# Filler matmuls in the light steps of a scan, a third slot for spread step sizes, and a reordered opening, in a language-model tower on one core

## The reference

```python
emb = tok_table[token_ids] + seg_table[segment_ids] + pos_table
h = layernorm(emb) * gamma + beta
x = layernorm(h)
# mamba block on x, h = h + block(x)
u = rmsnorm(x) * w_norm1
z = (u @ W_in.T) * sigmoid(u @ W_gate.T)
dt_in, Bm, Cm = split(z @ W_xproj.T, [96, 16, 16])
dt = softplus(dt_in @ W_dt.T + b_dt)
A_bar = exp(dt[..., None] * A);  Bx = (dt * z)[..., None] * Bm[:, :, None, :]
hs[t] = A_bar[t] * hs[t - 1] + Bx[t]          # along the 128 tokens, 384 channels x 16 states
y = sum_s(hs * Cm) + D_skip * z
x = x + y @ W_out.T
x = x + (silu(hf @ W_gate_ffn.T) * (hf @ W_up.T)) @ W_down.T       # hf = rmsnorm(x) * w
```

## Time and profile before

| what | us |
|---|---|
| three timed runs, median | 1767.92 |
| lowest and highest of them | 1763.59, 1771.11 |
| the profiled execution | 1750.55 |
| its span in the trace | 1748.8 |

### The profile page before, as it was taken

How to read it: one execution, slowest core, us unless ns; L and a number is a source line. 1 busy time by engine, 2 the same in 40 slices (tenths; PEclk the granted TensorE clock), 3 DMA queues, 4 the chain that set the end, 5 groups by cost and what they waited for, 6 DMA issues and landing times.

```text
span 1748.8 us, 22815 instructions
## 1 busy us (share of the span) xinstructions
PE 1333.2 (76%) x7000; PEld 914.0 (52%) x7000; DVE 807.0 (46%) x1503; ACT 522.6 (30%) x881; POOL 523.0 (30%) x421
## 2 busy tenths in 40 slices
PE   0437578889978776599994778989998889999960
PEld 0211123234233345499993564756657488888850
DVE  2337898776788664111111636355463422222212
ACT  0154455754744411133331213415151101001000
POOL 4645575644663561100113400000000600000025
PEclk9855677968787877799997668898988899999985
DMA  4233353442443312888982100000000388888843
GB/s 118 43 102 85 85 142 96 123 109 73 115 120 97 84 41 64 259 271 273 273 276 91 46 1 0 1 0 0 0 1 6 114 234 238 225 231 240 222 128 94
DMA packets 71612, 206.41 MB, mean 118 GB/s; under 512 B 11360, under 2 KB 32608, under 8 KB 66752
## 3 DMA queue, kind: packets, MB, share of 16 engines
q1 hardware_dynamic: 59648, 181.28, 37.3%
q0 software_dynamic: 11904, 24.40, 4.7%
HBM read 183.42 MB, written 22.22 MB: 118 GB/s over the span
## 4 chain that ended last, share of the span: by engine, by line
PE 43%; DMA 16%; DVE 15%; issue 9%; POOL 5%; ACT 4%; DVEq 2%; POOLq 2%; SPq 1%; ACTq 1%
PE ps L825 31%; DMA expert<-arena 13%; DVE arena L1479 4%; PE ps L956 3%; PE ps L1182 3%; POOL arena L546 2%; PE ps L970 1%; DMA arena<-sorted 1%; DMA arena<-dt 1%; PE ps L1174 1%; DVEq L1475 1%; DVE ps L1474 1%; ACT arena L687 1%; POOL h_rows L377 1%; PE ps L820 1%
## 5 line engine op out<-in xcount | busy, mean ns | idle before, releaser
L1479 DVE TENSOR_TENSOR_SCAN arena<-arena,ps 128x1024 f32<-128x1024 f32 x96 | 219.5, 2287 | 34.2 <-ACT arena L687 19.8
L825 PE MATMUL ps<-arena 96*128 96x128 f32 (+1 forms) x1680 | 222.5, 289 | 9.3 <-issue 8.2
L825 PE MATMUL ps<-xTF,wreg 96*128 96x512 f32 x352 | 217.3, 767 | 8.5 <-DVE arena L1648 4.6
L825 PEld LDWEIGHTS ps<-arena 96*128 96x128 f32 (+1 forms) x1680 | 213.6, 191 | 13.7 <-issue 13.7
L956 PE MATMUL ps<-arena,pick 32*128 32x512 f32 x384 | 134.6, 805 | 109.3 <-DVE arena L1479 97.7
L534 POOL DMA_DIRECT2D expert<-arena x88 | 47.7, 542 | 487.4 <-DVE arena L1608 268.1
L412 POOL DMA_INDIRECT sorted<-x_rows,row_i x64 | 62.8, 981 | 413.4 <-DVEq L1395 394.6
L687 ACT ACTIVATE arena<-arena,wreg 128x508 f32<-128x508 f32 x192 | 127.2, 710 | 118.5 <-DVE arena L1479 56.4
L825 PE MATMUL ps<-arena,ew_in 96*128 96x128 f32 x1248 | 150.0, 278 | 8.1 <-issue 7.8
L825 PEld LDWEIGHTS ps<-arena,ew_in 96*128 96x128 f32 x1248 | 145.6, 194 | 12.0 <-issue 11.9
L1474 DVE TENSOR_TENSOR ps<-ps,arena 128x1024 f32<-128x1024 f32 x96 | 117.1, 1219 | 73.9 <-PE ps L956 72.2
(11 more groups left out here) (208 smaller groups left out, 1723.6 us busy)
## 6 DMA issues: line engine op xcount, KB each, us to landing
arena<-dt SPq DMA_DIRECT2D x96, 512.0 KB, 4.6
ew_in<-in_e_in SPq DMA_DIRECT2D x24, 768.0 KB, 6.5
arena<-in_e_in SPq DMA_DIRECT2D x24, 768.0 KB, 6.2
ew_out<-in_e_out SPq DMA_DIRECT2D x20, 675.0 KB, 6.9
arena<-in_e_out SPq DMA_DIRECT2D x20, 675.0 KB, 7.1
...
```

What stands on the lines that cost most here:

```text
L825: last = pe.matmul(o, lhs, rhs, start=(n == 0), stop=(n == len(pairs) - 1))
L1479: ve.tensor_tensor_scan(hid[k % 3], dec[k % 3], bx.rearrange("p x t -> p (x t)"), 0.0, ALU.mult, ALU.add)\
```

## The change

Fillers: behind the jobs of a step, `keep_busy` counts what the step has on TensorE by a table of costs and adds matmuls of the identity with 256 columns of constants, up to 7 units; the results go to the bank of the next job and nobody reads them. A third `raw` slot lies in the upper half of what had been scratch (`ew_in_all[1]`), whose scratch tiles move up and get narrower. In chunk 0, VectorE multiplies z by the gate straight from PSUM, and ScalarE's copy and POOL's multiply go. POOL fetches chunk 1's rows at the start, and chunk 3's one tile at a time in steps 0 to 3. VectorE gets the mean square of the normalized rows as variance / (variance + eps), with no moments of their own. The embedding of chunks 2 and 3 stands at later steps, `embed_rows` of each chunk by itself.

```diff
-        raw = [part(18432, 1024), part(19456, 1024)]
+        raw = [part(18432, 1024), part(19456, 1024), ew_in_all[1][:, 0:1024]]
...
-        def rt(n, words=256):
-            return ew_in_all[1][:, 256 * n:256 * n + words]
+        def rt(n, words=192):
+            return ew_in_all[1][:, 1024 + 192 * n:1024 + 192 * n + words]
...
-                if k >= 2:
-                    sp.wait_ge(s_dec, 2 * (k - 1))
-                sp.dma_start(raw[k % 2], dt_rows[c][4 * g + i, half:half + 1].broadcast_to((NST, 8, 2 * CN))).then_inc(s_raw[k % 2], 16)
+                if k >= 3:
+                    sp.wait_ge(s_dec, 2 * (k - 2))
+                sp.dma_start(raw[k % 3], dt_rows[c][4 * g + i, half:half + 1].broadcast_to((NST, 8, 2 * CN))).then_inc(s_raw[k % 3], 16)
...
             embed(0)
+            embed(1)
             pool.wait_ge(s_sm, 4 * 16)
...
             embed_beta(0)
-            embed(1)
-            embed(2)
             pool.wait_ge(s_emb[1], 2 * CT * 16)
             embed_sum(1)
             embed_pos(1)
-            embed(3)
+            embed(2)
             pool.wait_ge(s_fn, 2)
             embed_gamma(1)
             embed_beta(1)
-            for g in range(DG):
-                gate_z(0, g)
...
                     if c == 0:
-                        if n == 1:
+                        if n < CT:
+                            embed(3, (n,))
+                        if n == 5:
                             pool.wait_ge(s_emb[2], 4 * CT * 16)
                             embed_sum(2)
-                        if n == 2:
+                        if n == 6:
                             embed_pos(2)
-                        if n == 3:
+                        if n == 8:
                             embed_sum(3)
-                        if n == 4:
+                        if n == 11:
                             embed_pos(3)
-                        if n == 8:
+                        if n == 14:
                             pool.wait_ge(s_fn, NCH)
                             embed_gamma(2)
-                        if n == 9:
+                        if n == 15:
                             embed_beta(2)
-                        if n == 10:
+                        if n == 20:
                             embed_gamma(3)
-                        if n == 11:
+                        if n == 21:
                             embed_beta(3)
...
             for job, _ in opening[:12]:
-                work(job)
+                if job[0] != "ez":
+                    work(job)
...
+            cost = dict(eturn=1, egate=4, ez=4, elow=6, edt=2, ebc=2, lout=6, lturn=1, lgate=4, lup=4, ldown=8, lnext=1, lrout=4,
+                        lscore=1, rank=1)
+            order = [(c, n, job) for c in range(NCH) for n in range(PAIRS) for job in work_at(c, n)]
+
+            def keep_busy(c, n, todo):
+
+                left = [job for cc, nn, job in order if (cc, nn) > (c, n)]
+                units = 7 - 2 - (2 if n % 2 else 0) - sum(cost[job[0]] for job in todo)
+                if not left or units <= 0:
+                    return
+                b = seat(*left[0])
+                for _ in range(units):
+                    pe.matmul(ps[:, b, 0:2 * P], ident, cst[:, 0:2 * P], start=True, stop=True)
...
                 for job in todo[1:]:
                     work(job)
+                keep_busy(c, n, todo)
...
-                norm(x, h_rows[:, c * CT:(c + n) * CT, :], LN_EPS, n=n * CT)
-                ve.drain()
-                moments(x, n * CT)
-                rstd(x_rms[:, c * CT:(c + n) * CT], n * CT, RMS_EPS, True)
+                m = n * CT
+                norm(x, h_rows[:, c * CT:(c + n) * CT, :], LN_EPS, n=m)
+                ve.drain()
+                ve.tensor_tensor(tt[:, 0:m], yy[:, 0:m], yy[:, 0:m], ALU.mult)
+                ve.drain()
+                ve.tensor_tensor(mv[:, 0:m, 1], tt[:, 0:m], mv[:, 0:m, 1], ALU.mult)
+                ve.drain()
+                rstd(x_rms[:, c * CT:(c + n) * CT], m, RMS_EPS, False)
...
+            for g in range(DG):
+                bank, n = seats["ez", 0, g]
+                ve.wait_ge(s_sig, g + 1)
+                ve.wait_ge(s_wfull[bank], n + 1)
+                ve.tensor_tensor(zT[0][:, g, :], ps[:, bank, :], tA[:, g, :], ALU.mult).then_inc(s_wfree[bank], 1)
+                ve.drain().then_inc(s_z, 1)
             embed_norm(1, 1)
             embed_rows(1, 1)
...
-                if k == 6:
+                if k == 12:
                     embed_norm(2, 2)
-                if k == 14:
-                    embed_rows(2, 2)
+                if k == 18:
+                    embed_rows(2, 1)
+                if k == PAIRS + 2:
+                    embed_rows(3, 1)
```

More of the change, by code:

```diff
@@ L203, in tower @@
         s_uf, s_dec, s_scan, s_hc, s_sum = [sem(n) for n in ("s_uf", "s_dec", "s_scan", "s_hc", "s_sum")]
[L204 removed]
+        s_raw, s_dtw = [sem(f"s_raw{k}") for k in range(3)], [sem(f"s_dtw{g}") for g in range(DG)]
         s_yT, s_yfree = sem("s_yT"), sem("s_yfree")
@@ L374, in _, with embed @@
             pool.wait_ge(s_idx, 32)
-            def embed(c):
-                for t in range(c * CT, (c + 1) * CT):
+            def embed(c, tiles=range(CT)):
+                for t in [c * CT + j for j in tiles]:
                     pool.indirect_dma_start(h_rows[:, t, :], None, tok_tab, bass.IndirectOffsetOnAxis(tok_i[:, t:t + 1], 0))\
```

7 lines of the change are left out of this document (3 added, 4 removed).

## The result

| | before | after |
|---|---|---|
| median of 20 runs each, us | 1768.22 | 1757.01 |
| lowest, highest | 1753.81, 1778.72 | 1738.46, 1769.39 |
| profiled execution, its span | 1750.55, 1748.8 | 1742.62, 1740.9 |
| first scan starts at | 113.51 | 99.75 |
| from scan 0 to scan 31 | 157.7 | 162.8 |

The ratio is 0.9939 [0.991, 0.9967]: 11 us faster, where 1756 was forecast. The traces agree with the sum: the last scan starts 10.5 us earlier, and the terms of the forecast (all of them up to that scan) gave -12.

What follows compares the result with a forecast made beforehand. The prediction saw no one bound: opening, VectorE's embedding stretches and TensorE's falling clock each had their own. Terms -17 + 3 + 6 - 4 = -12 us gave 1756 us against the 1767.92 median, range 1738 to 1773.

Steps and rivals of the forecast that it cites:

- Opening: Before the first scan: it starts 17 us earlier; ends -15 with `elow` at 1.2 GHz, -10 if POOL comes late.
- The part on z: Opening: z on VectorE behind each projection lets ScalarE take `elow` at 68.3 instead of 86.14, -17.8 us.
- row fetches: +2.3: Opening, POOL: chunk 1's fetches move ahead of chunk 0's sum, which starts 2.3 us later.
- mean square: -1.4: Opening, VectorE: three small operations taking 0.7 us replace moments and follow-up of 2.15 us, -1.4.
- Stretches: Embedding arithmetic between scans on VectorE: one norm, 10.0, and two row parts, 20.2, instead of 27.0 us: +3.2.
- Fillers and waits of steps 0 to 31: Chunk 0's scan: VectorE's waits sum to 28 us against 21.9, +6; ends 12 (-10) and 45 (+23).
- the clock falls anyway: Scan: each VectorE stretch still leaves TensorE idle for some 8 us, so its clock drops despite fillers.
- my case: The forecast itself: terms sum to -12 us, 1756 us, with TensorE's clock still falling behind VectorE's stretches; chance 0.46.
- rival 1: Scan: the clock holds, waits shrink to 12, softplus chain gains 8; middle -27 us, 1741; chance 0.22.
- rival 3: Light steps of chunk 0 and the last chunk: fillers at 1.2 GHz cost 25 us, +13 overall, 1781; chance 0.11.
- The other chunks' fillers: Chunks 1 to 3: few light steps, hidden by the stretches just before them; taken at nothing.
- the third slot: ScalarE's waits for spreads before the softplus, chunks 1 and 2 (1.84, 2.01 us), go: -4; ends 0 and -8.

Runs made afterwards that it cites:

- z_only: The kernel before with only z multiplied by its gate on VectorE straight from PSUM; one run, 1761.49 us.
- m_moments: The changed kernel with the moments of the normalized rows computed again; one run, 1763.68 us.
- f_nowait: The changed kernel without fillers in steps 16, 18 and 20 of chunks 1 and 2; ratio to before 0.9937 [0.9897, 0.9977].
- b_fillonly: The kernel before with only the fillers added; ratio to before 0.9879 [0.98, 0.9957], 4 runs, median 1752.92 us.
- l_first: The changed kernel without the three fillers ahead of step 3; one run, 1778.36 us.
- h_steps: The changed kernel with POOL's fetches, sums and positions reordered, norm behind step 8, both row parts in one stretch behind step 14; one run, 1739.83 us.
- c_rawtwo: The changed kernel with two slots for spread step sizes again; ratio to before 0.9951 [0.9922, 0.9979].

## Why the forecast was right, and where it was right by luck

**Opening (-17; measured -13.8).** The part on z was right: z_only has its first scan at 95.95, 17.6 us earlier (forecast 17.8), and `elow` at 2.4 GHz took 2.84 us. The step that failed is "row fetches: +2.3" with "mean square: -1.4", together 0.9 for the start of TensorE; its first projection came 4.4 us later. The fetches did cost 2.45 on POOL, but the position pass then came 2.68 instead of 0.82 behind the sum, +1.9. The mean square did save 1.5 (m_moments). But with chunk 1's rows there early, POOL's position pass over them fell on VectorE's chain and held one operation, 1.46 us for 0.17 (the row at 41.95), +1.3. That is 2.45 + 1.9 + 1.3 - 1.5, or 4.1 of the 4.4. Both surcharges had been put at nothing. The size of the first is in part chance: the gap is 1.47 to 3.46 us in the seven kernels with all eight fetches ahead of the sum, so the -13.8 of this trace was -11.7 to -14.4 in kernels with the same opening.

**Stretches (+3.2; measured +12.8).** The step that failed was to count the arithmetic only. Unheld, the three stretches would be 14.7 - 5.8 = 9.0, 13.5 - 4.1 = 9.4 and 11.5 - 2.0 = 9.5, together 27.9, even below the 30.2 that I took. What I left out is whom VectorE meets there: 5.8 us of waiting for POOL, whose passes I read as moved but not against VectorE's new step, and 6.1 us of held operations. The row of 2.16 us beside 2.35 had shown the second. By the rule of the Trainium skill's page the sum was to be 4 us worse; measured was 6.1 us, so the rule was nearer than leaving it out.

**Fillers and waits of steps 0 to 31 (+6; measured -7.7).** 162.8 - 108.8 - 39.8 = 14.2 us of waits, against 21.9 before and 28 forecast. By place: steps 3 to 6 4.8 (forecast 12), 7 to 12 0.2 (2), after step 12 1.2 (5), interval 18 and on 4.5 (2.5), after step 26 3.4 (6.5). The prices of one filler, 0.46 and 0.91, held. What failed is "the clock falls anyway": in chunk 0 it was 0.82, between my case and the 0.85 above which I would have called it rival 1. In chunk 0 that rival's mechanism ran; with a filler group ahead of step 3 it started there in eight of nine traces, and light steps up to 12 cost 3.55, not the 6.6 of rival 3. The wait of 3.1 us at interval 18 was not in the list: the softplus of chunk 0 had lain beside the old stretch and lost that cover.

**The other chunks' fillers (nothing; measured 0.1) and the third slot (-4; nothing there).** Scans 31 to 95 take 352.8 without fillers and 352.7 with them. That zero is a sum: intervals 86 and 90 gain 3.3 and 2.8, intervals 67 to 70 lose 7.1. f_nowait takes 3.7 of the 7.1 back, the price of the filler that waits for its bank and of the two behind it; the rest was not taken apart. I had costed fillers by their work and not by their waits. The zero is also luck: in b_fillonly, l_first and h_steps the same scans take 357.8 to 358.5, because the clock stayed low in scans 42 to 48. The third slot took both waits of the earlier trace rows away and shortened nothing behind them (c_rawtwo: 352.7 too); its 2.5 us stand in step 3, where the filler term had counted 2. The bound "0, if POOL's chain follows at once" was the right end. 1.8 us less than before remain for these chunks, which no run puts down to one part.

So the terms came out as -13.8 + 12.8 - 7.7 - 1.8 = -10.5, forecast -17 + 3 + 6 - 4 = -12. The sum was right to 1.5 us, while two of its terms were off by 10 and 14 us with opposite signs.

The last scan says the same of the parts: z_only has it at 615.9, the whole change at 615.2. What fetches, stretches, fillers and slot did beside z nearly cancels.

The time behind the last scan goes with how much the first mixture's loads move. The table by stage, 200 us of that stage, starting 50 us after the last scan, of the changed kernel and of z_only:

```profile
665.20:865.20 200.00, 155.95 (x1110) 147.01 (x1111) 36.23 (x124) 49.41 (x174) 22.09 (x34) 0.89 0.83 247
665.90:865.90 200.00, 149.26 (x1024) 138.77 (x1023) 35.91 (x124) 46.34 (x162) 20.46 (x31) 0.87 0.78 230
```

The code is the same there; 247 and 230 GB/s go with 1125.7 and 1143.9 us to the end. Why the loads differ was not settled.
